# Where the last two additions of a cross-attention kernel run: output rows finished on VectorE instead of ScalarE and GpSimd

## The reference

```python
q = _split_heads(hidden_states @ w_q, HEADS)
k = _split_heads(text @ w_k, HEADS)
v = _split_heads(text @ w_v, HEADS)
out_text = _merge_heads(_sdpa(q, k, v))
mask_ip = _ip_mask(bbox, B, S, hidden_states.dtype)
k_ip = _split_heads(ip_h @ w_k_ip, HEADS)
v_ip = _split_heads(ip_h @ w_v_ip, HEADS)
out_ip = _merge_heads(_sdpa(q, k_ip, v_ip, mask=mask_ip))
out = (out_text + out_ip) @ w_out + b_out
out = out + residual
```

## Time and profile before

| | us |
|---|---|
| median of 3 runs | 1375.77 (1375.22 to 1375.90) |
| the profiled execution | 1375.22 |
| its span, first to last instruction | 1373.0 |
| PE busy in the span | 1280.8 (93%) |
| DVE busy | 1036.1 (75%) |
| ACT busy | 883.5 (64%) |
| POOL busy | 1000.8 (73%) |

### The profile page before, as it was taken

One profiled execution on the slowest core, in us unless ns is written; L12 is line 12 of the kernel. 1 busy time (PEld: TensorE's weight loads), 2 busy tenths in 40 slices (PEclk: granted clock), 3 DMA queues, 4 the chain that ended last, 5 costly groups with the idle time before them and its releaser, 6 DMA issues.

```text
span 1373.0 us, 40303 instructions
## 1 busy us (share of the span) xinstructions
PE 1280.8 (93%) x15608; PEld 1214.6 (88%) x15608; DVE 1036.1 (75%) x2190; ACT 883.5 (64%) x1936; POOL 1000.8 (73%) x1166
## 2 busy tenths in 40 slices
PE   6697887489999999999999999999999999999986
PEld 5697787379999999999999999999999999999985
DVE  4265854378888888888888888888888888888872
ACT  2343444177777777777777777777777777777762
POOL 0132222068888888888888888888888888888885
PEclk9899989599999999999999999999999999999997
DMA  5588899534444444444444444444444444444421
GB/s 159 78 171 193 167 195 177 105 80 108 111 107 110 112 108 111 109 111 111 112 116 110 111 108 109 109 112 112 111 115 101 118 109 110 109 108 110 99 69 39
DMA packets 361277, 158.54 MB, mean 115 GB/s; under 512 B 298432, under 2 KB 350656, under 8 KB 359808
## 3 DMA queue, kind: packets, MB, share of 16 engines
q1 hardware_dynamic: 361088, 155.97, 50.8%
HBM read 91.85 MB, written 43.05 MB: 98 GB/s over the span
## 4 chain that ended last, share of the span: by engine, by line
PE 73%; POOL 3%; DVE 3%; issue 2%; ACT 1%; DMA 0%; POOLq 0%; DVEq 0%; SPq 0%
PE ps_o L913 18%; PE ps_b L839 14%; PE ps_a L839 11%; PE ps_s L882 8%; PE ps_s L888 8%; PE ps_m L858 7%; PE ps_a L931 3%; PE ps_a L828 2%; POOL prob_lo L1191 1%; PE ps_b L829 1%; PE ps_b L932 1%; PE ps_a L870 1%; POOL attn L1207 1%; DVE stats L1106 1%; POOL y L1198 1%
## 5 line engine op out<-in xcount | busy, mean ns | idle before, releaser
L1191 POOL TENSOR_TENSOR prob_lo<-prob,prob_hi 128x512 f16<-128x512 f32 (+1 forms) x448 | 524.6, 1183 | 89.6 <-ACT prob_hi L1037 89.5
L1036 ACT ACTIVATE prob<-ps_s 128x512 f32<-128x512 f32 (+1 forms) x448 | 254.4, 568 | 104.0 <-PE ps_s L888 100.9
L913 PE MATMUL ps_o<-values,prob_hi 128*128 128x64 bf16 (+7 forms) x4992 | 292.6, 194 | 4.2 <-DVE heads L1120 1.9
L913 PEld LDWEIGHTS ps_o<-values,prob_hi 128*128 128x128 f16 x4992 | 257.5, 98 | 34.4 <-DVE values L1138 17.0
L913 PE MATMUL ps_o<-values,prob_lo 128*128 128x68 bf16 (+7 forms) x3328 | 284.5, 195 | 0.0
L882 PE MATMUL ps_s<-q_hi_lo,keys 128*128 128x256 f32 x960 | 256.4, 303 | 0.0
L1037 ACT ACTIVATE prob_hi<-ps_s 128x512 f16<-128x512 f32 (+1 forms) x448 | 251.2, 561 | 0.0
L888 PE MATMUL ps_s<-q_hi_extra,keys 128*128 128x256 f32 x960 | 235.0, 281 | 0.8 <-ACT q_hi_extra L1026 0.8
L1106 DVE TENSOR_REDUCE stats<-ps_m 128x8 f32<-128x552 f32 x320 | 231.1, 722 | 0.2 <-issue 0.2
L1207 POOL TENSOR_TENSOR attn<-heads 128x128 f32<-128x128 f32 (+1 forms) x256 | 183.8, 718 | 55.5 <-DVE heads L1120 55.2
L913 PEld LDWEIGHTS ps_o<-values,prob_lo 128*128 128x128 f16 x3328 | 214.3, 98 | 0.0
(11 more groups left out here) (157 smaller groups left out, 3212.3 us busy)
## 6 DMA issues: line engine op xcount, KB each, us to landing
x_in<-in_x_dram SPq DMA_DIRECT2D x64, 320.0 KB, 3.0
q_hi_extra<-q_hi_lo SPq DMA_DIRECT2D x64, 320.0 KB, 3.4
x_keep<-in_x_dram SPq DMA_DIRECT2D x64, 320.0 KB, 3.1
out_dram<-y SPq DMA_DIRECT2D x128, 160.0 KB, 1.8
k_scratch<-k_stage SPq DMA_DIRECT2D x16, 770.0 KB, 5.8
keys<-k_scratch SPq DMA_DIRECT2D x256, 48.1 KB, 2.1
ctx_in<-in_ctx_dram SPq DMA_DIRECT2D x64, 128.0 KB, 3.1
v_scratch<-v_stage SPq DMA_DIRECT2D x64, 120.0 KB, 5.6
```

The lines of the kernel that those rows point to most:

```text
L913: last = mm(o[:, :, oo:oo + w], stat, v[:, :, a:a + w], start=first, stop=False, skip_group_check=True)
L1036: nc.scalar.activation(prob[:, s, 0:w], ps_s[RING[s]][:, 0:w], ACT.Exp)
L1191: nc.gpsimd.tensor_tensor(prob_lo[par(b)][:, s, 0:w], prob[:, s, 0:w], prob_hi[par(b)][:, s, 0:w], ALU.subtract).then_inc(s_lo, 1)
```

## The change

ScalarE's copy `y_out` is gone, and so is GpSimd's in-place `finish`. VectorE has a `finish(t)` of its own, which reads the product out of PSUM and `x_keep` out of SBUF and writes `y`. The semaphore `s_ye` is gone; TensorE now waits for `s_yr` in its place.

```diff
@@ tensor: x_transpose @@
                         if n is None or n >= 2:
-                            pe.wait_ge(s_ye, at(b, NT, -3 * NT))
+                            pe.wait_ge(s_yr, at(b, NT, -3 * NT))
@@ tensor: stats_transpose @@
-                            pe.wait_ge(s_ye, at(b, NT, 1 - 3 * NT))
+                            pe.wait_ge(s_yr, at(b, NT, 1 - 3 * NT))
@@ tensor: attn_transpose @@
-                            wait(pe, s_ye, b, NT, 0)
+                            wait(pe, s_yr, b, NT, 0)
@@ scalar @@
-                        def y_out(t):
-                            act.wait_ge(s_op, at(d, NT, t + 1))
-                            if t == 0 and (n is None or n >= 4):
-
-                                act.wait_ge(s_y[par(d)], nth(d, 32, -32))
-                            nc.scalar.copy(y[par(d)][:, t, :], (ps_a, ps_b)[t][:, 0:D]).then_inc(s_ye, 1)
@@ vector @@
+                        def finish(t):
+                            dve.wait_ge(s_op, at(d, NT, t + 1))
+                            if t == 0:
+                                dve.wait_ge(s_xb, at(d, 1, 1))
+
+                                reg = d[0] is not None
+                                if reg or d[1] >= 2:
+                                    dve.wait_ge(s_y[par(d)], nth(d, 32, -32))
+                            nc.vector.tensor_tensor(y[par(d)][:, t, :], (ps_a, ps_b)[t][:, 0:D], x_keep[par(d)][:, t, :],
+                                                    ALU.add).then_inc(s_yr, 1)
@@ vector, the list of a step @@
                         if Bs:
                             spread_values(0)
+                        if Ds:
+                            finish(0)
                         if A:
                             maxima(2)
+                        if Ds:
+                            finish(1)
                         if Bs:
                             spread_values(1)
@@ gpsimd @@
-                        def finish(t):
-                            pool.wait_ge(s_ye, at(d, NT, t + 1))
-                            if t == 0:
-                                pool.wait_ge(s_xb, at(d, 1, 1))
-                            nc.gpsimd.tensor_tensor(y[par(d)][:, t, :], y[par(d)][:, t, :], x_keep[par(d)][:, t, :],
-                                                    ALU.add).then_inc(s_yr, 1)
```

More of the change, by code:

```diff
@@ L699, in xattn_kernel @@
             s_yr = sem("y_ready")
-            s_ye = sem("y_evacuated")
             s_xk = [sem(f"residual_loaded{q}") for q in range(2)]
@@ L1045, in step @@
                             exps(1)
-                        if Ds:
-                            y_out(0)
-                        if Bs:
                             exps(2)
-                        if Ds:
-                            y_out(1)
-                        if Bs:
                             exps(3)
@@ L1185, in step @@
                         E, A, Bs, Cs, Ds = has(n)
-                        a, c, d = off(b, 1), off(b, -1), off(b, -2)
+                        a, c = off(b, 1), off(b, -1)
                         def rest(s):
@@ L1240, in step @@
                             rest(4)
-                        if Ds:
-                            finish(0)
-                            finish(1)
                         if Cs:
```

## The result

| | before | after |
|---|---|---|
| median of the runs, us | 1375.64 (4 runs, 1375.22 to 1375.90) | 1388.38 (4 runs, 1388.08 to 1392.24) |
| ratio | | 1.0099, 95% interval 1.0082 to 1.0117 |
| the profiled execution, and its span | 1375.22, 1373.0 | 1391.13, 1389.3 |
| first `spread_values` of two steps, 59 steps apart | 311.26, 1304.94 | 312.20, 1324.16 |
| one step | 16.84 | 17.15 |

The changed kernel is 12.7 us slower; the forecast was 13.5. The spans differ by 16.3, in three stretches: 0.9 ahead of the first of these steps, 59 x 0.31 = 18.3 in them, and -2.9 behind the last (68.1 us before, 65.1 after). The profiled execution of the changed kernel lies 2.8 above the median of its runs, so the spans overstate the loss.

The account below looks back on a forecast made before the run. TensorE bounds the kernel, in a loop with ScalarE and VectorE tight in four places. 60 steps x 0.30 = 18.0 us lost, less 4.5 at the end, gives +13.5: 1389.3 us, range 1374 to 1404 for 8 in 10.

Parts of the forecast that it names:

- The additions: On VectorE, two additions a step from PSUM, 0.41 us each from start to start, bounds 0.41 to 0.49.
- The meeting with `rest`: `spread_values(1)` meets GpSimd's third `rest`, ends 0.65 us behind it, and `maxima(3)` starts 0.44 late.
- rival 1: At `spread_values(1)`: VectorE is not held by `rest`; `maxima(3)` 0.19 late, 1374.3 us, no difference; chance 0.16.
- What TensorE gets back: At `project(e, 0)`, 0.14 of the 0.44 us; nothing at `sum_heads(0)`; each full step 0.30 longer.
- Rival 2: At `max_scores(4)`: VectorE's 0.54 us of idle takes up everything, steps stay 16.84, total 1371.3; chance 0.09.
- Rival 3: At `x_transpose`: additions take 0.49 and its wait passes to `x_lo`; 0.56 us a step, 1404.9; chance 0.18.
- Rival 4: `spread_values(1)` misses the end of `rest`, POOL's bias addition goes first; another 1.5 us a step, near 1479; chance 0.04.
- The last steps: At the end, without POOL's additions: 1.7, 1.97 and 0.87 us less, 4.5 in sum, bounds 0.87 to 4.5.
- the forecast's sign: In the last steps' trace, the last `attn_transpose` should not wait for POOL's second pair of additions, worth 1.97 us.
- The sum: Whole kernel: 18.0 us lost in 60 full steps less 4.5 at the end, +13.5, giving 1389.3.

Follow-up runs that it names:

- e1: Changed kernel, with GpSimd's third `rest` of a step waiting until the second `spread_values` is done: 1375.77 us, ratio 1.0001.
- e4: Changed kernel, with only the second addition of a step on VectorE, the first staying on ScalarE and GpSimd: 1390.16 us, ratio 1.0107.
- e3: Kernel before, with `sum_heads(c, 2)` moved ahead of `max_scores(a, 4)` in TensorE's list: 1375.75 us, ratio 1.0006.
- e6: Changed kernel, with two small VectorE reductions between `finish(1)` and `spread_values(1)` in 60 steps: 1555.82 us, ratio 1.1318.
- e5: Kernel before, with the additions moved to VectorE only in the last four steps (62 to 65): 1371.64 us, ratio 0.9980.
- e9: Kernel before, with `sum_heads(c, 2)` ahead of `max_scores(a, 4)` and `scores(b, 6)` ahead of `project(e, 0)` on TensorE: 1372.95 us, ratio 0.9979.
- e10: Changed kernel, `sum_heads(c, 2)` before `max_scores(a, 4)`, `scores(b, 6)` before `project(e, 0)`, GpSimd's third `rest` waiting for `spread_values(1)`: 1356.22 us, ratio 0.9861.

## Why the prediction was right

- **The additions.** 0.41 from start to start was forecast; the rows show 0.40 (827.45 to 827.85, 828.62 to 829.02), 0.48 long. `maxima(2)` 0.77: 0.77.
- **The meeting with `rest`.** Forecast: `rest` 1.17, `spread_values(1)` ends 0.65 behind it. Measured: `rest` 1.16 from 828.24, `spread_values` ends at 830.04, 0.64 behind. `maxima(3)` starts 3.20 behind the first `spread_values`; forecast 3.22. e1 and e4 show it as the cause. So rival 1, which left this out, was wrong. e1 comes near to the kernel that it had in mind, but makes GpSimd wait: it gave 1374.3, and e1 ran at 1375.8.
- **One thing moved that was not forecast:** GpSimd's loss. `rest` no longer takes 1.78, but the bias addition behind it takes 2.10 in place of about 1.5, held by the same `spread_values`. Nothing waits for it.
- **What TensorE gets back.** 0.14 at `project(e, 0)`, nothing at `sum_heads(0)`: both hold, and `attn_transpose` still waits for `q_lo`. 0.30 a step was forecast, 0.31 is measured. The forecast reached it by a lateness of 0.44 (from where the load stood before) less 0.14, wait by wait; e3 shows the simpler reason, a chain with 0.30 of waiting in it in any case, and what exceeds that counts: 0.58 less 0.30.
- **Rival 2** had this half: a shift within that 0.30 is nearly free, as e1 shows (a lateness of 0.32 costs 0.05). The shift was larger.
- **Rival 3** fell: `x_lo` was not delayed, and the additions overlap.
- **Rival 4** did not happen in the changed kernel, by 0.4 us; e6 makes it happen, at its forecast 1.5 a step while the clock is full. What the sum for it left out was the clock.
- **The last steps** are the mis-sized term: 4.5 was forecast, 3.6 is measured by e5's runs (0.7 to 4.8 by their interval, so the runs alone would allow 4.5), and by the two traces the terms are 1.26 for 1.7, 1.08 for 1.97 and 0.84 for 0.87, 3.2 in all. The first falls short because `max_scores(4)` waits 1.17 in that step too, where it waited 0.75 before. The second does because GpSimd stays what `attn_transpose` waits for, 2.04 in place of 2.85: VectorE's `finish` delays the last long `spread_values`, which then meets GpSimd, takes 1.39, and makes the bias addition 2.09 long in place of 1.55. So the forecast's sign, that this `attn_transpose` should not wait for the second pair, holds to the letter only: the pair is gone, and GpSimd is still late.
- **Left out of the sum** was the clock, here as in rival 4: in the last steps the granted clock falls in the traces of both kernels, of e3 and of e5 (0.50 in the last 11 to 12 us of both kernels), and e3's end is 2.4 longer than that of the kernel before.
- **The sum.** By the traces 18.3 + 0.9 - 2.9 = 16.3, by the medians 12.7. The profiled executions lie 2.8 above and 0.4 below their medians, so the parts do not add up to 12.7. The forecast's own terms, 18.0 - 4.5, come by the traces to 18.6 (60 steps) - 3.2 = 15.4; that 13.5 is within 0.8 of the medians' 12.7 is in part luck. The start of the first of the 59 steps, where the change does nothing, lies between 308.10 (e9) and 313.61 (e10) in the profiled executions, which is more than this difference.

## What to carry to other kernels

In this kernel an in-order engine had no spare time to offer but the gap at the one place where its next result was due; 16% of idle time elsewhere bought nothing. When work is moved onto an engine, look at what its next instruction will meet on the other engines at its new time: here the meeting cost more than the work (0.26 of the 0.31 us a step). And judge a change together with the order of the engine that waits: the same change lost 13 us in the given order, and is worth 20 us once two products of TensorE are moved, since then, by e9's trace, GpSimd, which it relieves, would be the late one.

## What the runs showed of the hardware

- A VectorE product of two SBUF inputs (128x1200, bf16) that meets a GpSimd instruction on SBUF ends 0.64 to 0.65 behind it, whenever it began: 0.77 alone, 1.02, 1.12, 1.39 and 1.76 in the rows above. The other way round the GpSimd instruction grew by 0.5 to 0.6 (1.17 to 1.78, 1.55 to 2.10). The Trainium skill, "SBUF — State Buffer", section "Who interferes with whom", has them take turns as wholes; these rows agree, save that what is left behind the GpSimd instruction's end is 0.13 less than the 0.77 that the product takes alone.
- VectorE's additions with one input in PSUM took 0.48 with GpSimd busy on SBUF beside them (the one at 828.62 lies inside the `rest` from 828.24), which agrees with the same section's exception.
- TensorE's clock: waits of 0.5 once a step left it at 1.00 (the window of the changed kernel); with waits of 2.0 once a step (e6) 48 of 59 steps had a mean of 0.92 (a fall to 0.50 for somewhat over 3 us in the rows above), which cost 1.26 a step in the mean beside the 1.5 of the longer wait.
